# Delta projection of a state-space layer: scan work put between the sigmoids, one logarithm and one store in place of sixteen

## The chip, the cores and the metric

The program runs on all 8 cores of one Trainium2 chip. Each core takes one half of the sequence of one of the four batch rows, and runs the same instructions; nothing is exchanged between cores. The time is the device time of the slowest core, in microseconds (us). TensorE (PE) multiplies matrices, VectorE (DVE) does elementwise work and recurrences, ScalarE (ACT) does the activation functions, GpSimd (POOL) only issues stores here, and SyncE (SP) only issues loads. Each engine runs its own instructions in the order in which the program lists them.

## The reference, cut to what matters

```
x_and_res = x @ in_proj_w                       # 1024 -> 2 x 2048
h = silu(conv1d(xp) + conv_b)                   # depthwise, 4 taps
x_dbl = h @ x_proj_w                            # -> dlt (64), B (16), C (16)
delta = softplus(dlt @ dt_proj_w + dt_proj_b)   # 2048 channels
state_t = exp(delta_t * A) * state_{t-1} + delta_t * h_t * B_t
y = (state . C + h * D) * silu(res);   x1 = layernorm(x + y @ out_proj_w)
out = layernorm(x1 + shared_mlp(x1) + sum over the top 2 of 16 experts(x1))
```

The input is (4, 8192, 1024). The change touches only how `delta` is made and stored. The program keeps minus delta: ln(sigmoid(-v)) is -softplus(v).

## The kernel before, in words

A core owns 4096 tokens, but it also computes h, delta, B and C for the 4096 tokens ahead of them, since it needs the state with which its own half begins (a flag sets that state to zero on cores that hold the first half). The program has these stages, with a barrier of all engines between them: weights are cast to bf16; stage A makes h, delta, B, C and silu(res) for 32 slabs of 256 tokens (`SLAB`), the first 16 not owned, the last 16 owned; the scan stage runs the recurrence over the owned half; then output projection, norm, router, and the experts. Stage A runs from about 1014 us to the scan stage.

One slab of stage A goes as follows. SP loads x (L385 casts it on DVE). Then 16 column blocks, 32 where the slab is owned: PE multiplies (L403), DVE copies and does the four taps (L415 to L432), ACT applies Silu into `a_h` (L437); in an owned slab the second 16 blocks give silu(res), one activation (L445) and one store each. POOL stores h in one transfer of 2 MB. PE multiplies h by the 96 columns of `x_proj` (L455), ACT copies dlt, B and C out (L461, L464), POOL stores B and C. Then the part that is changed, which I call the delta part: a loop of 16 blocks with a matmul (L473) and a Sigmoid (L477) each, and a loop of 16 blocks with a Ln (L483) into one tile `a_dl` and a store to `d_delta` each. Ahead of each Ln, `QS.wait_all(sc)` makes ACT wait until all stores issued so far have landed, and so until `a_dl` may be written again.

Beside the slabs runs a generator, `gen_bp`, which works out what the half that is not owned leaves in the state. One instance covers 512 tokens, two slabs. Each call of `pump()` puts its next piece into the program at that point, on all engines. An instance has 16 pieces that spread B over the partitions (L311, L316), and then five for each of the 16 channel blocks (`dc`): the first loads delta and h, makes `b_u`, a running sum and `b_Dp` on DVE (L327, L329, L333), one small Exp (L337) and a group of four; the next three are a group of four each; the fifth adds to `sb_acc` (L362). A group of four is four Exp of 512 columns on ACT (L345), four products on DVE (L349) and four more with a sum (L355). The Exps of a group wait until the products L349 of the group before are done, by a wait of ACT on DVE. With the call that finds it finished, an instance takes 97 calls.

Before, `pump()` is called once ahead of each column block (16 or 32 calls a slab). An instance is made at the end of each odd slab among the first 16; what is left of it two slabs later is pumped out at once, which I call the drain (65 of 97 calls). The last instance, made after slab 15, has no drain and is worked off in the owned slabs 16 to 19. There are thus seven pairs of slabs with a drain (2 and 3 up to 14 and 15), and the first slab of a pair I call even, the second odd.

Of the kernel before, what the change touches and what calls it, by code (L numbers as in the profile page):

```python
# [11 lines left out]
AF = mybir.ActivationFunctionType  # L12
# [4 lines left out]
NDC = DIN // 128  # L17
NKC = DIM // 128
NF = 72
SLAB = 256  # L20
# [78 lines left out]
def build(T_OWN=4096, debug=False):  # L99
# [24 lines left out]
    out = nc.dram_tensor("out", [T_OWN, DIM], F32, kind="ExternalOutput").ap()  # L124
# [6 lines left out]
    def interior(name, shape, dt):  # L131
        return nc.dram_tensor(name, shape, dt, kind="Internal").ap()
# [6 lines left out]
    d_delta = interior("d_delta", [128, NDC, T2], F32)  # L139
# [39 lines left out]
    cx = Ctx(nc, es)  # L179
    te, sc, ve, sy, gp = nc.tensor, nc.scalar, nc.vector, nc.sync, nc.gpsimd  # L180
    QL = DmaQ(cx, sy, "qL", 8)
    QS = DmaQ(cx, gp, "qS", 8)

    with nc.Block() as blk:
        TE, SC, VE = "pTE", "pSC", "pVE"
# [79 lines left out]
        TE, SC, VE = "aTE", "aSC", "aVE"  # L265
# [8 lines left out]
        a_dl = A32.take(SLAB)  # L274
        a_sig = A32.take(NDC * SLAB)
# [94 lines left out]
        def pump():  # L370
            if pend[0] is not None:
                try:
                    next(pend[0])
                except StopIteration:
                    pend[0] = None
        for sl in range(2 * NS):
            t0 = sl * SLAB
# [4 lines left out]
                in_=x_fm_all[:, :, 8 + t0 - 3: 8 + t0 + SLAB].rearrange("k p c -> p k c"))  # L382
# [3 lines left out]
                                      in_=a_xfm.rearrange("p (k c) -> p k c", k=8)[:, :, 0:259]))  # L386
            x16_ready = cx.val(VE)
            m_list = list(range(16)) + (list(range(16, 32)) if owned else [])
            for mi, m in enumerate(m_list):
                pump()  # L390
                gi = (mi // 4) % 2
                if mi % 4 == 0:
                    cx.wait_val(sy, TE, wtb_free[gi])
                    QL.dma(out=wtb[gi].rearrange("p (k mc) -> p k mc", k=8),
                        in_=d_winb.rearrange("p (k mc) -> p k mc",
                                             k=8)[:, :, m * 128:(m + 4) * 128])
# [13 lines left out]
                if m < 16:  # L410
# [27 lines left out]
                                             in_=a_cv[1][:], func=AF.Silu,  # L438
                                             bias=sb_cb[:, dc:dc + 1]))
                    cv_rel[mi % 2] = cx.val(SC)  # L440
                else:
# [7 lines left out]
                                            in_=a_sil[:])  # L449
            cx.wait(gp, SC)  # L450
            QS.dma(out=d_h[:, :, t0:t0 + SLAB],
                                    in_=a_h.rearrange("p (d c) -> p d c", d=NDC))
# [14 lines left out]
            QS.dma(out=d_B[:, t0:t0 + SLAB], in_=a_bc[64:80, :])  # L467
            QS.dma(out=d_C[:, t0:t0 + SLAB], in_=a_bc[80:96, :])
            sig_rel = [0, 0]
            for m in range(NDC):  # L470
                pdt = pD if m % 2 == 0 else pC
                cx.wait_val(te, SC, max(sig_rel[m % 2], dlt_ready))
                cx.inc(TE, te.matmul(pdt[:, 0:SLAB], sb_wdt[:, m * 128:(m + 1) * 128],  # L473
                                     a_dlt[0:64, :], start=True, stop=True))
                cx.wait(sc, TE)
                cx.wait(sc, SC)
                cx.inc(SC, sc.activation(out=a_sig[:, m * SLAB:(m + 1) * SLAB], in_=pdt[:, 0:SLAB],  # L477
                                         func=AF.Sigmoid, scale=-1.0, bias=sb_ndtb[:, m:m + 1]))
                sig_rel[m % 2] = cx.val(SC)
            for m in range(NDC):  # L480
                QS.wait_all(sc)
                cx.wait(sc, SC)
                cx.inc(SC, sc.activation(out=a_dl[:], in_=a_sig[:, m * SLAB:(m + 1) * SLAB],  # L483
                                         func=AF.Ln))
                cx.wait(gp, SC)
                QS.dma(out=d_delta[:, m, t0:t0 + SLAB], in_=a_dl[:])

            if sl % 2 == 1 and sl < NS:
                while pend[0] is not None:
# [14 lines left out]
        TE, SC, VE = "oTE", "oSC", "oVE"  # L504
# [20 lines left out]
        for sl in range(NSB):  # L525
            t0 = T_OWN + sl * SLB
# [3 lines left out]
            for g in range(NST):  # L530
# [7 lines left out]
                                         in_=(pA if g % 2 == 0 else pB)[:, 0:SLB],  # L538
                                         func=AF.Copy))
            cx.wait(sy, TE)  # L540
            QL.dma(out=o_state[0:1, 0:NST * SLB], in_=d_C[:, t0:t0 + SLB])
            for g in range(NST):
# [7 lines left out]
                                         in_=(pA if g % 2 == 0 else pB)[:, 0:SLB],  # L550
                                         func=AF.Copy))
            for dc in range(NDC):
# [11 lines left out]
                for n0 in range(0, NST, 4):  # L564
                    cx.wait_val(sc, VE, dA_free[0])
                    for j in range(4):
                        cx.inc(SC, sc.activation(  # L567
                            out=o_dA[j][:], in_=o_dl[bb], func=AF.Exp,
                            scale=sb_negA[:, dc * NST + n0 + j:dc * NST + n0 + j + 1]))
                    cx.wait(ve, SC); cx.wait(ve, VE)  # L570
                    for j in range(4):
                        cx.inc(VE, ve.scalar_tensor_tensor(  # L572
                            out=o_dBu[j][:], in0=o_u[:], scalar=1.0,
# [3 lines left out]
                    for j in range(4):  # L577
                        n = n0 + j
                        cx.inc(VE, ve.tensor_tensor_scan(  # L579
                            out=o_state[:, n * SLB:(n + 1) * SLB], data0=o_dA[j][:],  # L580
# [5 lines left out]
                    for j in range(4):  # L586
                        n = n0 + j
                        cx.inc(VE, ve.scalar_tensor_tensor(  # L588
                            out=o_prod[j][:], in0=o_state[:, n * SLB:(n + 1) * SLB],
# [14 lines left out]
                    else:  # L604
# [8 lines left out]
                                          in_=o_state[:, SLB - 1::SLB]))  # L613
# [20 lines left out]
        TE, SC, VE = "cTE", "cSC", "cVE"  # L634
# [12 lines left out]
        for sl in range(NS):  # L647
            t0 = sl * SLAB
            cx.wait(sy, TE); cx.wait(sy, VE); cx.wait(sy, SC)
            QL.dma(out=c_y1.rearrange("p (d c) -> p d c", d=NDC),  # L650
                                    in_=d_y1[:, :, t0:t0 + SLAB])
            QL.dma(out=c_x.rearrange("p (a c) -> p a c", a=2),
                                    in_=x_own[t0:t0 + SLAB, :].rearrange("(a p) c -> p a c", p=128))
# [16 lines left out]
            for tc in range(2):  # L670
# [3 lines left out]
                for nh in range(2):  # L674
# [40 lines left out]
                                        in_=x1tc)  # L715
                for kc in range(NKC):
# [6 lines left out]
                        out=c_fm32[:, kc * SLAB + tc * 128:kc * SLAB + tc * 128 + 128],  # L723
                        in_=pC[:, 0:128], func=AF.Copy))
# [5 lines left out]
                                    in_=c_fm16.rearrange("p (k c) -> p k c", k=NKC))  # L730
            for tc in range(2):
                cx.wait(te, SC)
                for k in range(NKC):
# [52 lines left out]
                                         in_=pC[0:16, 0:128], func=AF.Copy))  # L786
# [4 lines left out]
        if debug:  # L791
            tmp = A32t[:, 0:DIM]
            for sl in range(NS):
                t0 = sl * SLAB
                for tc in range(2):
# [4 lines left out]
                                            in_=tmp)  # L800
# [4 lines left out]
                                        in_=tmp[0:16, 0:SLAB])  # L805
            stage_barrier([])

        TE, SC, VE = "dTE", "dSC", "dVE"
# [16 lines left out]
        for sl in range(NSD):  # L825
            t0 = sl * SLD
            cx.wait(sy, TE); cx.wait(sy, VE)
            QL.dma(out=g_x1.rearrange("p (k c) -> p k c", k=NKC),
                   in_=d_x1fm[:, :, t0:t0 + SLD])
            QL.dma(out=g_cwf[0:1, :], in_=d_cw[:, t0:t0 + SLD])  # L830
            for pe in range(18):
                pp = pe % 2
                f0 = pe * 4
                for g in range(2):
                    cx.wait_val(sy, TE, gwt_free[g][pp])
                    QL.dma(out=g_wt[g][pp].rearrange("p (k f c) -> p k f c", k=8, f=4),
                           in_=d_wgub.rearrange("g p (k ff c) -> g p k ff c",
                                                k=8, ff=NF)[g, :, :, f0:f0 + 4, :])
# [52 lines left out]
        TE, SC, VE = "eTE", "eSC", "eVE"  # L891
# [9 lines left out]
        for sl in range(NS):  # L901
            t0 = sl * SLAB
            cx.wait(sy, VE); cx.wait(sy, SC)
            QL.dma(out=e_x1.rearrange("p (a c) -> p a c", a=2),
                                    in_=d_x1[t0:t0 + SLAB, :].rearrange("(a p) c -> p a c", p=128))
            for half in range(2):
# [3 lines left out]
                                        in_=d_z[:, half * 36:(half + 1) * 36, t0:t0 + SLAB])  # L910
                for kk in range(36):
                    k = half * 36 + kk
                    gi2 = (kk // 2) % 2
                    if kk % 2 == 0:
                        cx.wait_val(sy, TE, ewd_free[gi2])
                        QL.dma(out=e_wd[gi2].rearrange("p (a c) -> p a c", a=2),
                               in_=d_wdownb[k:k + 2].rearrange("a p c -> p a c"))
# [17 lines left out]
            for tc in range(2):  # L935
# [3 lines left out]
                for nh in range(2):  # L939
# [24 lines left out]
                                         func=AF.Sqrt, scale=1.0 / DIM, bias=sb_tiny[:, 4:5]))  # L964
# [15 lines left out]
                                        in_=otc)  # L980
# [84 lines left out]
```

How the kernel before makes its waits and increments, by code:

```python
    def inc(self, name, instr, k=1):  # L39
        instr.then_inc(self.sem(name), k)
        self.ledger[name] += k
        return instr
# [4 lines left out]
    def wait_val(self, eng, name, v):  # L47
        if v <= 0:
            return
        key = (id(eng), name)
        if self.waited.get(key, -1) >= v:
            return
        eng.wait_ge(self.sem(name), v)
        self.waited[key] = v
```

## Time and profile before

| What | Value |
|---|---|
| Median of 3 runs | 26255.3 us (26250.2 to 26335.7) |
| The profiled execution's own time | 26236.4 us |
| Its span, first to last instruction, slowest core | 26234.9 us |
| Busy DVE / PE / ACT / POOL, share of the span | 45% / 28% / 19% / 4% |
| One pair of slabs with drain, 2058.3 to 2833.3 us | 775.0 us |
| One owned slab without a generator, from one store of h to the next | 188.3 us |

The span is that of the slowest of 8 cores (26186.8 to 26234.9 us). "Busy" counts an engine's own work, not its waits; in brackets behind a row of a timeline stands how long the engine stood idle ahead of it, and which engine or transfer ended that. No engine is busy half of the time, so the time lies in waits, and it has to be read stage by stage.

### The profile page before, as it was taken

The numbers are of one execution on the slowest core, as the hardware profiler recorded it, in microseconds if no ns is written. First come the engines' busy times: TensorE is split into PE (matmuls) and PEld (weight loads), VectorE is DVE, ScalarE is ACT, GpSimd is POOL, SyncE is SP. The second block draws the span as 40 slices with busy tenths as digits, with TensorE's granted clock in tenths as the row PEclk, the third lists the DMA queues.
The fourth block names the chain that finished last, engine by engine and source line by source line (L and its number), as shares of the span: only waits on it lengthen the run. The fifth ranks groups of instructions, "written<-read, shape, count | busy, mean of one in ns | idle before, by whom it ended". The sixth has DMA issues, their size and how long they took to land.

```text
span 26234.9 us, 118127 instructions; the slowest of 8 cores (26186.8 to 26234.9 us)
## 1 busy us (share of the span) xinstructions
PE 7269.4 (28%) x24864; PEld 3115.4 (12%) x24864; DVE 11884.3 (45%) x19992; ACT 5004.7 (19%) x8360; POOL 966.0 (4%) x1734
## 2 busy tenths in 40 slices
PE   0112211102234442000000000000233577775444
PEld 0101100001112221000000000000111233332111
DVE  1255565655532124877877878778200122220000
ACT  0033333333431111111111111111111111110000
POOL 0000000000001110000000000000000011100000
PEclk9855555555555555555555555555555688988888
DMA  5411111011122221000000000000111233334555
GB/s 207 146 35 39 38 35 40 30 32 37 52 65 82 87 82 42 15 14 14 16 13 14 16 13 15 15 13 16 50 59 59 92 127 126 124 127 153 165 169 163
DMA packets 1154022, 1729.76 MB, mean 66 GB/s; under 512 B 66272, under 2 KB 780512, under 8 KB 1141984
## 3 DMA queue, kind: packets, MB, share of 16 engines
q1 hardware_dynamic: 1039360, 1349.58, 16.3%
q0 software_dynamic: 113952, 372.62, 3.9%
q8 instruction: 213, 3.49, 0.1%
q14 instruction: 497, 4.07, 0.1%
HBM read 1349.44 MB, written 372.51 MB: 66 GB/s over the span
## 4 chain that ended last, share of the span: by engine, by line
DVE 40%; DMA 27%; PE 11%; ACT 11%; issue 9%; DVEq 1%; SPq 0%; ACTq 0%; POOLq 0%; POOL 0%
DVE A L579 9%; DMA d_z<-A 6%; DMA A<-d_wdownb 5%; DVE A L588 5%; DVE A L572 5%; ACT A L345 5%; DVE A L349 5%; DMA d_delta<-A 4%; DMA A<-d_woutb 3%; PE pO L924 3%; DMA d_silu<-A 2%; DVE A L355 2%; PE pO L663 2%; DVE A L593 1%; DVE A L874 1%
## 5 line engine op out<-in xcount | busy, mean ns | idle before, releaser
L579 DVE TENSOR_TENSOR_SCAN A<-A,sb_carry 128x512 f32<-128x512 f32 x2048 | 2463.0, 1264 | 55.0 <-DVE A L572 1.8
L567 ACT ACTIVATE A<-A,sb_negA 128x512 f32<-128x512 f32 x2048 | 1310.2, 710 | 6097.5 <-DVE A L579 3485.4
L532 PE MATMUL pA<-A,sb_ones 1*128 1x512 f32 x128 | 130.7, 1122 | 6746.3 <-DMA A<-d_B 6699.4
L349 DVE SCALAR_TENSOR_TENSOR A<-A 128x512 f32<-128x512 f32 x2048 | 1278.9, 687 | 1561.4 <-ACT A L345 1561.4
L572 DVE SCALAR_TENSOR_TENSOR A<-A 128x512 f32<-128x512 f32 x2048 | 1279.1, 686 | 642.6 <-ACT A L567 601.7
L924 PE MATMUL pO<-A 128*128 128x512 bf16 x4608 | 1173.7, 403 | 1282.9 <-DMA A<-d_wdownb 1282.8
L403 PE MATMUL pA<-A 128*128 128x259 bf16 x3072 | 713.9, 412 | 2665.0 <-DMA A<-d_winb 1288.6
L345 ACT ACTIVATE A<-A,sb_A 128x512 f32<-128x512 f32 x2048 | 1307.7, 709 | 738.1 <-DVE A L349 736.8
L854 PE MATMUL pO<-A 128*128 128x512 bf16 x4608 | 1238.0, 417 | 546.5 <-DVE A L874 545.2
L355 DVE SCALAR_TENSOR_TENSOR A<-A 128x512 f32<-128x512 f32 x2048 | 1295.2, 689 | 54.3 <-DVE A L349 0.9
L870 DVE SCALAR_TENSOR_TENSOR A<-pO,A 128x512 f32<-128x512 f32 x512 | 354.2, 692 | 2100.2 <-DMA d_z<-A 1772.6
L588 DVE SCALAR_TENSOR_TENSOR A<-A 128x512 f32<-128x512 f32 x2048 | 1279.1, 687 | 54.9 <-DVE A L579 1.8
L403 PE MATMUL pB<-A 128*128 128x259 bf16 x3072 | 715.5, 412 | 1698.5 <-DVE A L415 1405.3
L863 PE MATMUL pO<-A 128*128 128x512 bf16 x4608 | 1164.0, 398 | 0.0
L311 PE MATMUL pO<-A,sb_ones 1*128 1x512 f32 x256 | 262.0, 1125 | 2873.7 <-DMA A<-d_B 2441.7
L941 DVE TENSOR_TENSOR A<-pO,A 128x512 f32<-128x512 f32 x64 | 44.3, 692 | 2238.4 <-PE pO L924 1933.9
L663 PE MATMUL pO<-A 128*128 128x512 bf16 x1024 | 477.4, 620 | 1803.0 <-DMA A<-d_woutb 1803.0
L532 PEld LDWEIGHTS pA<-A,sb_ones 1*128 1x128 f32 x128 | 31.8, 307 | 6844.3 <-issue 6844.3
L860 ACT ACTIVATE A<-pO 128x512 f32<-128x512 f32 x576 | 344.0, 597 | 2234.6 <-PE pO L854 2234.6
L403 PEld LDWEIGHTS pA<-A 128*128 128x128 bf16 x3072 | 395.7, 138 | 3050.9 <-issue 2902.2
L676 DVE TENSOR_TENSOR A<-pO,A 128x512 f32<-128x512 f32 x64 | 44.3, 692 | 1515.9 <-PE pO L663 1185.8
L385 DVE CAST A<-A 128x2072 bf16<-128x2072 f32 x32 | 39.8, 1242 | 1522.5 <-DMA A<-x_fm_all 1522.5
(146 smaller groups left out, 11420.2 us busy)
## 6 DMA issues: line engine op xcount, KB each, us to landing
A<-d_wgub SPq DMA_DIRECT2D x288, 1024.0 KB, 8.0
A<-d_wdownb SPq DMA_DIRECT2D x576, 512.0 KB, 3.7
A<-d_winb SPq DMA_DIRECT2D x192, 1024.0 KB, 6.4
A<-wgu_f SPq DMA_DIRECT2D x36, 2048.0 KB, 7.2
d_z<-A POOLq DMA_DIRECT2D x576, 128.0 KB, 2.0
A<-d_z SPq DMA_DIRECT2D x32, 2304.0 KB, 14.6
d_h<-A POOLq DMA_DIRECT2D x32, 2048.0 KB, 9.0
d_delta<-A POOLq DMA_DIRECT2D x512, 128.0 KB, 2.0
```

Of the source, the lines that this page charges most:

```text
L345: cx.inc(BSC, sc.activation(out=b_E[j][:], in_=b_Dp[:], func=AF.Exp, scale=sb_A[:, dc * NST + n0 + j:dc * NST + n0 + j + 1]))
L349: cx.inc(BVE, ve.scalar_tensor_tensor(out=b_w[j][:], in0=b_E[j][:], scalar=1.0, in1=b_u[:], op0=OP.mult, op1=OP.mult))
L355: cx.inc(BVE, ve.scalar_tensor_tensor(out=b_wb[j][:], in0=b_w[j][:], scalar=1.0, in1=b_brep[:, (n0 + j) * SLB:(n0 + j + 1) * SLB], op0=OP. ...
L403: ins = te.matmul(ps[:, 0:259], wtb[gi][:, (k * 4 + mi % 4) * 128:(k * 4 + mi % 4 + 1) * 128], x16[:, k * 264:k * 264 + 259], start=(k == ...
L567: cx.inc(SC, sc.activation(out=o_dA[j][:], in_=o_dl[bb], func=AF.Exp, scale=sb_negA[:, dc * NST + n0 + j:dc * NST + n0 + j + 1]))
L572: cx.inc(VE, ve.scalar_tensor_tensor(out=o_dBu[j][:], in0=o_u[:], scalar=1.0, in1=o_brep[:, (n0 + j) * SLB:(n0 + j + 1) * SLB], op0=OP.mul ...
L579: cx.inc(VE, ve.tensor_tensor_scan(out=o_state[:, n * SLB:(n + 1) * SLB], data0=o_dA[j][:], data1=o_dBu[j][:], initial=sb_carry[:, dc * NS ...
L588: cx.inc(VE, ve.scalar_tensor_tensor(out=o_prod[j][:], in0=o_state[:, n * SLB:(n + 1) * SLB], scalar=1.0, in1=o_crep[:, n * SLB:(n + 1) * ...
L663: ins = te.matmul(pO[tc * 2 + nh][:, 0:512], c_y1[:, k * SLAB + tc * 128:k * SLAB + tc * 128 + 128], wb[:, nh * 512:(nh + 1) * 512], start ...
L854: ins = te.matmul(pg[:, 0:SLD], g_wt[0][pp][:, (k * 4 + f) * 128:(k * 4 + f + 1) * 128], g_x1[:, k * SLD:(k + 1) * SLD], start=(k == 0), s ...
L863: ins = te.matmul(pu[:, 0:SLD], g_wt[1][pp][:, (k * 4 + f) * 128:(k * 4 + f + 1) * 128], g_x1[:, k * SLD:(k + 1) * SLD], start=(k == 0), s ...
L924: ins = te.matmul(pO[tc * 2 + nh][:, 0:512], e_z[hb][:, kk * SLAB + tc * 128:kk * SLAB + tc * 128 + 128], wb[:, nh * 512:(nh + 1) * 512], ...
```

## The change: one wait moved, 20 more pieces a slab, one logarithm and one store

Ahead of the Sigmoid loop ACT now waits for all stores. In the loop each block begins with a `pump()`; one more follows the loop, then a single Ln over all 16 blocks (4096 columns, in place in `a_sig`), a single store of 2 MB, and three more calls of `pump()`. A slab thus makes 20 more calls while a generator is alive.

```
             QS.dma(out=d_C[:, t0:t0 + SLAB], in_=a_bc[80:96, :])
             sig_rel = [0, 0]
+            QS.wait_all(sc)
             for m in range(NDC):
+                pump()
                 pdt = pD if m % 2 == 0 else pC
...
                 sig_rel[m % 2] = cx.val(SC)
-            for m in range(NDC):
-                QS.wait_all(sc)
-                cx.wait(sc, SC)
-                cx.inc(SC, sc.activation(out=a_dl[:], in_=a_sig[:, m * SLAB:(m + 1) * SLAB],
-                                         func=AF.Ln))
-                cx.wait(gp, SC)
-                QS.dma(out=d_delta[:, m, t0:t0 + SLAB], in_=a_dl[:])
+            pump()
+            cx.wait(sc, SC)
+            cx.inc(SC, sc.activation(out=a_sig[:, :], in_=a_sig[:, :], func=AF.Ln))
+            cx.wait(gp, SC)
+            QS.dma(out=d_delta[:, :, t0:t0 + SLAB],
+                   in_=a_sig.rearrange("p (d c) -> p d c", d=NDC))
+            pump(); pump(); pump()
```

On ACT, in the delta part of slab 2 (the first even slab), the two copies of dlt, B and C (L461, L464), then the Sigmoids stood in a row before:

```order
L461 ACTIVATE A<-pC 64x256 [waits aTE,qS0,aSC]
L464 ACTIVATE A<-pC 32x256 [waits aSC]
L477 ACTIVATE A<-pD,sb_ndtb 128x256 [waits aTE,aSC]
L477 ACTIVATE A<-pC,sb_ndtb 128x256 [waits aTE,aSC]
L477 ACTIVATE A<-pD,sb_ndtb 128x256 [waits aTE,aSC]
```

The Sigmoids waited for TensorE alone (aTE) and for ACT's own last write. Now, in the same kind of place in the odd slab 3 (the Sigmoid is L479 now, bVE is the generator's DVE):

```order
L461 ACTIVATE A<-pC 64x256 [waits aTE,qS6,aSC]
L464 ACTIVATE A<-pC 32x256 [waits aSC]
L345 ACTIVATE A<-A,sb_A 128x512 [waits qS0,qS7,bVE]
L345 ACTIVATE A<-A,sb_A 128x512 x3
L479 ACTIVATE A<-pD,sb_ndtb 128x256 [waits aTE,aSC]
L345 ACTIVATE A<-A,sb_A 128x512 [waits bVE]
L345 ACTIVATE A<-A,sb_A 128x512 x3
L479 ACTIVATE A<-pC,sb_ndtb 128x256 [waits aTE,aSC]
```

Groups of four Exps stand between the Sigmoids; the wait for the two stores (qS0, qS7) is ahead of the first group, and the Sigmoids' own waits are the same as before. At the end of the same delta part ACT now has this row of work, the last Sigmoid, a group, the one Ln (L484), and groups again:

```order
L479 ACTIVATE A<-pC,sb_ndtb 128x256 [waits aTE,aSC]
L345 ACTIVATE A<-A,sb_A 128x512 [waits bVE]
L345 ACTIVATE A<-A,sb_A 128x512 x3
L484 ACTIVATE A<-A 128x4096 [waits aSC]
L345 ACTIVATE A<-A,sb_A 128x512 [waits bVE]
L345 ACTIVATE A<-A,sb_A 128x512 x3
L337 ACTIVATE A<-sb_negA,A 128x16 [waits bVE,bSC]
L345 ACTIVATE A<-A,sb_A 128x512 x4
```

The Ln waits for nothing but ACT itself, and the group behind it waits for the generator's DVE and for no store. On DVE, at the end of slab 2's taps (L432), stood the cast of the next slab's x (L385), and only then the first piece of a channel block (L327 to L333):

```order
L432 SCALAR_TENSOR_TENSOR A<-A,sb_cw 128x256 [waits aVE]
L385 CAST A<-A 128x8x259 [waits qL0,qL1,qL2,qL3,qL4,qL7,aVE]
L327 SCALAR_TENSOR_TENSOR A<-A 128x512 [waits qL5,qL6]
L329 SCALAR_TENSOR_TENSOR A<-sb_ones,A 128x512
L333 TENSOR_SCALAR A<-A 128x512 [waits bVE]
```

Now the piece stands right behind the taps, with four channel blocks ahead of the cast:

```order
L432 SCALAR_TENSOR_TENSOR A<-A,sb_cw 128x256 [waits aVE]
L327 SCALAR_TENSOR_TENSOR A<-A 128x512 [waits qL0,qL1,qL2,qL3,qL4,qL5,qL7]
L329 SCALAR_TENSOR_TENSOR A<-sb_ones,A 128x512
L333 TENSOR_SCALAR A<-A 128x512 [waits bVE]
L340 TENSOR_TENSOR A<-sb_acc,A 128x16 [waits bSC]
L349 SCALAR_TENSOR_TENSOR A<-A 128x512 [waits bSC,bVE]
```

DVE has the same instructions in all; they only stand elsewhere. (The order's name for L329 is that of the profile's TENSOR_TENSOR_SCAN.)

## Rows read from the trace of the kernel before

**Rows 1.** Windows: us, busy (xinstructions) of PE, PEld, DVE, ACT, POOL; PEclk; DMA; GB/s

```profile
2058.28:2833.25 774.97, 142.06 (x416) 70.67 (x416) 441.38 (x1011) 259.39 (x418) 21.74 (x38) 0.51 0.11 36
6874.60:7253.60 379.00, 85.82 (x326) 48.49 (x325) 186.04 (x428) 164.83 (x229) 19.59 (x36) 0.51 0.17 51
7253.60:7624.30 370.70, 84.14 (x318) 47.14 (x317) 180.17 (x416) 159.71 (x223) 19.56 (x36) 0.51 0.17 51
7813.60:8001.90 188.30, 81.30 (x318) 46.24 (x317) 39.11 (x81) 33.11 (x69) 19.47 (x35) 0.54 0.27 83
```

**Rows 2.** Waits of ACT, 1010 to 9480 us: us in total, times, longest

```profile
ACT A L483 <- DMA d_delta<-A: 1322.2, 420, 9.6
```

**Rows 3.** Timeline of ACT, slab 21: start, us, what, [idle before <-releaser]

```profile
8201.27 0.38 ACT L461 ACTIVATE A<-pC 64x256 f32<-64x256 f32 x1 [12.20 <-DMA d_h<-A]
8201.74 0.38 ACT L464 ACTIVATE A<-pC 32x256 f32<-32x256 f32 x1
8203.58 1.28 ACT L477 ACT_TABLE_LOAD   x1 [1.47 <-PE pD L473]
...
8220.00 1.28 ACT L483 ACT_TABLE_LOAD   x1
8221.29 0.42 ACT L483 ACTIVATE A<-A 128x256 f32<-128x256 f32 x1
8228.22 0.42 ACT L483 ACTIVATE A<-A 128x256 f32<-128x256 f32 x1 [6.51 <-DMA d_delta<-A]
...
8278.87 1.28 ACT L437 ACT_TABLE_LOAD   x1 [2.70 <-DMA d_delta<-A]
```

**Rows 4.** Timeline of POOL, the same slab: stores as they are issued

```profile
8191.90 1.14 POOL L75 DMA_DIRECT2D d_h<-A  x1 [1.70 <-issue]
...
8203.23 0.50 POOL L75 DMA_DIRECT2D d_C<-A  x1
```

**Rows 5.** Timeline of DVE, the slab after it: end of its second block's taps

```profile
8235.98 0.48 DVE L432 SCALAR_TENSOR_TENSOR A<-A,sb_cw 128x256 f32<-128x256 f32 x1
```

**Rows 6.** The page's DMA issues: KB each, us from issue to landing

```profile
d_C<-A POOLq DMA_DIRECT2D x32, 16.0 KB, 1.7
```

**Rows 7.** Groups of ACT by line, whole span: busy, mean ns of one, idle before

```profile
L681 ACT ACTIVATE A<-A 128x1024 f32<-128x1024 f32 x32 | 33.8, 1056 | 1420.0 <-DVE A L676 1420.0
```

**Rows 8.** Timeline of DVE and ACT in the drain of slab 7

```profile
3323.11 2.50 DVE L349 SCALAR_TENSOR_TENSOR A<-A 128x512 f32<-128x512 f32 x4 [0.18 <-ACT A L345]
...
3328.44 2.50 DVE L349 SCALAR_TENSOR_TENSOR A<-A 128x512 f32<-128x512 f32 x4 [0.19 <-ACT A L345]
...
3336.53 0.31 ACT L337 ACTIVATE A<-sb_negA,A 128x16 f32<-128x16 f32 x1 [8.26 <-DVE A L333]
...
3339.46 2.50 DVE L349 SCALAR_TENSOR_TENSOR A<-A 128x512 f32<-128x512 f32 x4 [2.34 <-ACT A L345]
...
3363.52 0.31 ACT L337 ACTIVATE A<-sb_negA,A 128x16 f32<-128x16 f32 x1 [8.27 <-DVE A L333]
```

**Rows 9.** Timeline of ACT, slabs 4 and 5: delta parts and taps

```profile
2144.13 0.38 ACT L464 ACTIVATE A<-pC 32x256 f32<-32x256 f32 x1
...
2219.04 0.42 ACT L483 ACTIVATE A<-A 128x256 f32<-128x256 f32 x1 [2.72 <-DMA d_delta<-A]
2219.36 0.29 ACT L337 ACTIVATE A<-sb_negA,A 128x16 f32<-128x16 f32 x1
...
2233.44 2.56 ACT L345 ACTIVATE A<-A,sb_A 128x512 f32<-128x512 f32 x4
2244.16 1.28 ACT L437 ACT_TABLE_LOAD   x1 [8.16 <-DVE A L432]
...
2245.98 1.28 ACT L345 ACT_TABLE_LOAD   x1
2247.28 2.56 ACT L345 ACTIVATE A<-A,sb_A 128x512 f32<-128x512 f32 x4
...
2420.61 0.38 ACT L464 ACTIVATE A<-pC 32x256 f32<-32x256 f32 x1
```

## The prediction

> **What bounds the kernel now.** I read the slices of the page first: DVE is the busiest engine at 45%, so the span is made of waits. Then I cut stage A into windows. A pair of slabs with a drain takes 775.0 us, of which DVE works 441 and ACT 259; an owned slab without a generator takes 188.3 us, with DVE at 39 and ACT at 33 [rows 1]. In both most of the time belongs to no engine. The list of ACT's waits names the owner of much of it: ACT waited 1322 us, 420 times, for a `d_delta` store to land before it could write the next Ln into the one tile [rows 2]. The timeline of one delta part shows the pattern: a Ln of 0.42 us, then a wait of 2.7 to 6.5, sixteen times; from the table load of the Ln to that of the next slab's Silu 58.9 us go by [rows 3]. The last view is the drain, where DVE is full: groups follow each other every 5.33 us (3323.11 to 3328.44), of which 0.19 are idle, and a channel block takes 26.99 us (3336.53 to 3363.52) [rows 8]. So there are three kinds of place: delta parts with no generator, where only latency is lost; delta parts with one alive, during which DVE's generator work could run; and drains, which DVE bounds and which get shorter by what is done earlier.
>
> The sum is made against the profiled execution, 26236.4 us (span 26234.9). That is 19 us under the median of the runs, which I add at the end.
>
> **Term 1: 16 delta parts with no generator work beside them** (slabs 0, 1 and 18 to 31; slab 18 still had pieces before, and they come under term 3).
> Before: from the end of L464 (8202.12) to the Silu's table load (8278.87), 76.75 us [rows 3].
> After, step by step:
> - The wait for the B and C stores now stands ahead of the Sigmoids. The second is issued at 8203.23, 1.1 us after L464 ends, and such a store lands in 1.7 [rows 4, 6], so the first table load comes after 2.8; I take 3.0 where it was 1.47. Cost 1.5.
> - The Sigmoid loop is the same, 8203.58 to 8220.00: 16.4.
> - Ln: load 1.28, then 4096 columns. 256 columns take 0.42 [rows 3] and 1024 take 1.06 [rows 7], so 0.83 us for 1000 columns, and 3.6 for all. Together 4.9, of which sixteen small ones would have used 6.7 for the same columns; the gain is in the waits.
> - The store: 0.6 to its issue (the first half of the 1.1 above, which holds two issues), then as the store of h, which has the same shape and size: issued at 8191.90, ACT released at 8201.27, 9.4 us [rows 3, 4]. That one ran nearly alone. This one meets the loads of the next slab's x and weights. Their price can be bounded by the first Ln wait after them, 6.51 where the last is 2.70 [rows 3]: 3.8, and I allow nearly twice that, 7, since this store has sixteen times the bytes. So 9.4 to 16.4; I take 14, near the upper end, since all of it falls among these loads.
> Sum 3.0 + 16.4 + 4.9 + 0.6 + 14 = 38.9, and 76.75 − 38.9 = 37.8; I use 37.5, with 35 to 42.5 as ends. Next in line are the taps of the slab that follows: two blocks of them were ready at 8236.46, 16.5 us after the Sigmoids ended (8220.00) [rows 3, 5], and the Silu now comes 19.5 after them. So the taps are just not late; if the store were quicker than 11 us, they would be what ends the wait. For slab 1 (whose end is followed by a wait of SP) and slab 31 (followed by the barrier), the loads matter less: 42 each. Term 1: 14 × 37.5 + 2 × 42 = 609 us.
>
> By the Trainium skill (DMA: Bandwidth & Descriptors, section Anatomy of one DMA — SWDGE (gpsimd) path) such a store takes 2.0 us plus its bytes over 436 KB per us, 6.8 us for 2 MB. The row above has 9.4, so it does not agree; by the rule term 1 would be about 42 us larger.
>
> **Term 2: seven pairs with a drain.** The generator's pieces are only moved: 20 into the even slab, 20 into the odd, 40 fewer in the drain. In the delta part a group now stands between two Sigmoids. The Sigmoid waits for TensorE and not for DVE, so ACT does its table load and the Sigmoid (1.28 + 0.47) while DVE does its four products L349 (2.50); that is hidden. Not hidden is the load ahead of the next Exps, since it comes behind the wait for these products: 1.28, with the gap 1.30 (2245.98 to 2247.28) [rows 9]. A group costs 5.33 + 1.30 = 6.63, and a channel block with four such loads 27.0 + 5.2 = 32.2. No load stands between a Ln and an Exp (2219.04, 2219.36) [rows 9]. The single Ln, 4.9 us, stands where ACT else waits 2.8 for DVE, so it costs 2.1. Whether Exp next to Sigmoid needs a load is not in the trace; each costs 0 or 1.3 by the rows, and I take 1.3 as between Silu and Exp.
> Even slab, from the end of L464 to the first Exp of the fifth block (L337): before 2144.51 to 2219.36, 74.9. After: store wait 3.0; three blocks 96.6; the fourth with two loads and the Ln 27.0 + 2.6 + 2.1 = 31.7; the cast of x, which is now in DVE's row of work, 1.3. Sum 132.6. Cost 57.7. The odd slab's taps begin at the same piece as before, so they take the same time.
> Odd slab, from the end of L464 (2420.99) to the end of the pair (2833.25): before 412.3 [rows 1, 9]. After: wait 3.0; first group to its products 1.3 + 2.6 + 0.2 = 4.1; from there to the next L337, two groups (2 × 5.33) and 8.1 (3328.44 to 3336.53), plus 2.6 of loads, 21.4; two blocks 64.4; one with three loads and the Ln 33.0; five in the drain 135.0; less 2.1, because the drain ends ahead of the next block's first steps. Sum 258.8. Gain 153.5.
> A pair gains 95.8; I use 95: term 2 is 665 us.
>
> **Term 3: slabs 16 to 18.** Slab 16's delta part now takes 20 pieces. From L464 to the first group of slab 17 it is 3.0 + 4.1 + 21.4 + 64.4 + 33.0 + 5.5 (from L337 over its own group to the next, 2.9 + 2.6) = 131.4, against 74.9 in the like part before: cost 56.5. Slab 17 takes 32 pieces in its blocks as before (379.0 and 370.7 us for such slabs [rows 1]), and the last 12 in its delta part: wait 3.0, group 4.1, to L337 8.1, a block 32.2, the last block to its fourth products 2.9 + 1.3 + 3 × 6.63 = 24.1, the last Sigmoids 6, Ln 4.9, issue and store 14, so 96.4, 20 more than 76.75. Slab 18 is then free of pieces: 188.3 + 20 in place of 370.7, gain 162. Term 3: 162 − 56.5 = 106; I use 105.
>
> Sum: 609 + 665 + 105 = 1379. 26236.4 − 1379 = 24857, plus 19: 24876, and I say 24880 us, 5.2% faster. The later stages have the same instructions, and the scan stage is bound by DVE; I give them nothing. The change leaves ACT with 480 fewer Ln and POOL with 480 fewer stores; beyond the waits counted above I give that nothing.
>
> **A rule that speaks against this.** In the row, a load of 1.28 at 2244.16, a Silu and a load of 1.28 at 2245.98 are all done by 2247.28: 3.12 us, which leaves 0.56 for the Silu and every gap [rows 9]. So a switch costs 1.3 here. The Trainium skill (ScalarE: Activation LUTs, section What ACT_TABLE_LOAD costs) puts a switch at 2.66 us, 1.38 of it a drain beside the load. By the rule each load on the path would cost twice as much; the time is that of the third rival.
>
> **The rivals.**
> - *The moved pieces gain nothing* (terms 2 and 3 are zero, term 1 stands): stalls that I don't see, of loads for the generator behind the next x in SP's queue or of stores, eat 95 us a pair. For it: ACT is ordered, and the generator was slow in the taps. Against it: the delta part has no DVE work of its own. Time 26255 − 609 = 25646.
> - *The delta part runs at the pace of the taps, and the kernel is slower.* In the taps a group takes 13.84 us (2233.44 to 2247.28), because ACT's Silu waits for DVE (8.16 idle at 2244.16) and the next Exps stand behind it [rows 9]. If the Sigmoid were held as long, a group would cost 7.2 more. 26 groups a pair and 22 in term 3 are 204 groups: 1469 us, more than 1379. Time 26255 + 90 = 26345. It decides from 6.63 + 1379/204 = 13.4 us a group. Against it: the Sigmoid's wait is on TensorE, whose matmul is ready two blocks ahead.
> - *A switch costs 1.38 us more in the delta part*, by a drain of ACT that the Silu rows don't show. On the path are 28 loads a pair (14 in each slab) and 23 in term 3: 219 × 1.38 = 302. Time 25180.
> - *Exp and Sigmoid need no load between them*: 219 × 1.3 = 285 us more gain. Time 24595.
>
> **How the numbers follow.** My forecast 0.83, nothing from the moved pieces 0.05, slower 0.03, dearer switches 0.05, no loads 0.04. My own terms have these ends: term 1 from 560 to 680, term 2 from 75 to 105 us a pair, so 525 to 735, and with term 3 as it is they leave 24735 to 25065. The range 24730 to 25100 holds these and leaves the rivals out. A measurement of this kernel tells about 0.3% (79 us) from no change. Faster by more than that: all but the slower rival and a small rest, 0.95; within 0.3%: 0.02; slower 0.03.
>
> **What would show it.** One Ln of 3.6 us a slab, and ACT's wait for `d_delta` gone from 1322 us to some 10 us in 14 to 16 places, now ahead of a Silu. In the delta parts of slabs 2 to 17, DVE's products L349 every 6.6 us with a table load of L345 ahead; a spacing of 5.3 would speak for the last rival, 8 for the third, 13 for the second. A pair of 680 us, with a drain of 25 pieces. An owned slab without generator of 151 us. If slabs without generator don't get shorter by 35 or more, the wait on the store was not what held them, and the forecast fails at its first term.

## The result: 5.6% faster, and the profile after

| | before | after |
|---|---|---|
| Median of 8 runs each | 26266.2 us | 24803.7 us |
| Ratio, 95% interval | | 0.9441 [0.9431, 0.9451] |
| Profiled execution, its span | 26236.4, 26234.9 us | 24812.4, 24810.6 us |
| ACT's wait for `d_delta` stores inside the delta part, core 4, all of stage A | 1502 us, 476 times | none |

The forecast was 24880 us; the measured time is 76 us lower and inside the range. The slowest core was core 2 before and is core 4 after; so that two dies are not mixed up, I compare core 4 of both. [rows 2] are of core 2 and end at 9480 us, before the stage does, hence the 1322 us there. On core 4 the waits of ACT before, and what is left after, now ahead of the next slab's Silu:

```profile
ACT A L483 <- DMA d_delta<-A: 1502.2, 476, 8.7
...
ACT L437 <- DMA d_delta<-A: 133.2, 10, 16.6
```

The prediction had 14 to 16 such places of some 10 us. There are 10, of 13.3 us on average; in most of the other delta parts without a generator DVE's taps end the wait, which the prediction called just not late.

The stage can be cut at the stores of h. The timeline of POOL on core 4 before, at slabs 2, 16, 18 and 31:

```profile
1364.24 1.14 POOL L75 DMA_DIRECT2D d_h<-A  x1 [77.50 <-ACT A L437]
...
6863.07 1.18 POOL L75 DMA_DIRECT2D d_h<-A  x1
...
7608.71 1.18 POOL L75 DMA_DIRECT2D d_h<-A  x1
...
10032.68 1.14 POOL L75 DMA_DIRECT2D d_h<-A  x1 [1.70 <-issue]
```

and after, at the same four slabs:

```profile
1282.58 1.13 POOL L75 DMA_DIRECT2D d_h<-A  x1 [85.92 <-ACT A L437]
...
6105.30 1.13 POOL L75 DMA_DIRECT2D d_h<-A  x1 [0.56 <-issue]
...
6742.37 1.17 POOL L75 DMA_DIRECT2D d_h<-A  x1
...
8640.36 1.17 POOL L75 DMA_DIRECT2D d_h<-A  x1
```

The differences give the account, beside what the prediction had for each piece (slab 0's own store of h stands at 1075.9 before and 1070.2 after; the first matmul of the scan stage at 10117.2 and 8688.7):

| Stretch, core 4 | before | after | gain | predicted |
|---|---|---|---|---|
| h of slab 0 to h of slab 2 | 288.4 | 212.4 | 76.0 | 79.5 (term 1) |
| slab 2 to slab 16 (the seven pairs) | 5498.8 | 4822.7 | 676.1 | 665 (term 2) |
| slab 16 to slab 18 | 745.6 | 637.1 | 108.5 | 105 (term 3) |
| slab 18 to slab 31 | 2424.0 | 1898.0 | 526.0 | 487.5 (term 1) |
| slab 31 to the scan stage | 84.5 | 48.3 | 36.2 | 42 (term 1) |

With the 5.7 us ahead of slab 0, which the change does not touch (that store stands anywhere from 1060 to 1076 in the ten profiles), stage A got 1428.5 us shorter, where 1379 was forecast. The stages behind it took 9 us longer in this execution, with the same instructions. The windows of the kernel after (core 4; columns as in [rows 1]) for a pair, the slabs from 16 and from 17, and an owned slab without generator:

```profile
1614.03:2289.16 675.13, 144.80 (x417) 70.52 (x416) 441.47 (x1010) 317.19 (x438) 6.61 (x8) 0.51 0.13 41
...
6105.30:6538.18 432.88, 85.61 (x321) 47.51 (x320) 274.81 (x636) 235.46 (x307) 11.94 (x20) 0.51 0.16 49
6538.18:6742.37 204.19, 85.21 (x322) 47.89 (x321) 92.42 (x208) 75.30 (x109) 12.70 (x21) 0.53 0.25 80
6888.77:7033.72 144.95, 81.10 (x322) 46.28 (x321) 39.40 (x81) 30.08 (x54) 11.98 (x22) 0.56 0.34 109
```

DVE's work in a pair is what it was in [rows 1] (441 us), so the 100 us by which this pair is shorter were idle time of DVE. ACT has 20 more instructions, with 30 fewer Ln, so 50 more table loads: 64 us, less 6 for the Lns, and its work grew from 259 to 317. The delta part of a slab without generator, on ACT (answers to [rows 3]):

```profile
6898.09 0.38 ACT L464 ACTIVATE A<-pC 32x256 f32<-32x256 f32 x1
6901.46 1.28 ACT L479 ACT_TABLE_LOAD   x1 [3.00 <-DMA d_C<-A]
...
6917.89 1.28 ACT L484 ACT_TABLE_LOAD   x1
6919.18 3.62 ACT L484 ACTIVATE A<-A 128x4096 f32<-128x4096 f32 x1
6936.29 1.28 ACT L437 ACT_TABLE_LOAD   x1 [13.49 <-DMA d_delta<-A]
```

From the end of L464 (6898.47) to the Silu's load are 37.8 us; 38.9 was forecast and 76.75 stood there before. Over the 13 slabs from 18 to 30 the mean is 37.8, where it was 77.5 before; a store ends the wait in nine of them and the taps in four. The Ln takes 3.62 where 3.6 was worked out, the wait for the small stores 3.00 where I took 3.0. And with a generator alive, on ACT at the end of slab 4's delta part (answers to [rows 8, 9]):

```profile
2072.63 0.47 ACT L479 ACTIVATE A<-pC,sb_ndtb 128x256 f32<-128x256 f32 x1
2074.07 1.28 ACT L345 ACT_TABLE_LOAD   x1 [0.96 <-DVE A L349]
2075.36 2.56 ACT L345 ACTIVATE A<-A,sb_A 128x512 f32<-128x512 f32 x4
2077.82 3.60 ACT L484 ACTIVATE A<-A 128x4096 f32<-128x4096 f32 x1
2081.33 2.54 ACT L345 ACTIVATE A<-A,sb_A 128x512 f32<-128x512 f32 x4
```

and DVE a little ahead of it:

```profile
2052.59 2.50 DVE L349 SCALAR_TENSOR_TENSOR A<-A 128x512 f32<-128x512 f32 x4 [1.46 <-ACT A L345]
...
2059.19 2.50 DVE L349 SCALAR_TENSOR_TENSOR A<-A 128x512 f32<-128x512 f32 x4 [1.46 <-ACT A L345]
```

The products follow each other every 6.60 us (6.63 was forecast), idle 1.46 in place of 0.19: a table load stands ahead of each group of Exps. The Ln has none ahead of it when it follows an Exp, which I had not seen coming (the load before the Exps already brings the logarithm); it saves 1.3 us in each such delta part.

### The profile page after: what moved, and what is told of

Same layout as the page of the kernel before. It is cut to its first block, busy times and chain, and to the rows that moved or that the text cites. A ratio compares the mean times of both kernels' runs of the same rounds, so it can differ in the third digit from the quotient of the medians.

```text
span 24810.6 us, 115616 instructions; the slowest of 8 cores (24748.5 to 24810.6 us)
## 1 busy us (share of the span) xinstructions
PE 7561.1 (30%) x24864; PEld 3166.4 (13%) x24864; DVE 11887.1 (48%) x19992; ACT 5347.4 (22%) x8224; POOL 725.2 (3%) x1254
## 4 chain that ended last, share of the span: by engine, by line
DVE 43%; DMA 24%; PE 12%; ACT 12%; issue 8%; DVEq 1%; SPq 0%; ACTq 0%; POOLq 0%; POOL 0%
DVE A L581 10%; DMA d_z<-A 6%; DMA A<-d_wdownb 6%; DVE A L590 5%; DVE A L574 5%; DVE A L349 5%; ACT A L345 5%; DMA A<-d_woutb 3%; PE pO L926 3%; DMA d_silu<-A 2%; DVE A L355 2%; PE pO L665 2%; DVE A L595 1%; DVE A L876 1%; DVE A L872 1%
## 5 line engine op out<-in xcount | busy, mean ns | idle before, releaser
L926 PE MATMUL pO<-A 128*128 128x512 bf16 x4608 | 1184.0, 405 | 1299.7 <-DMA A<-d_wdownb 1299.4
L856 PE MATMUL pO<-A 128*128 128x512 bf16 x4608 | 1344.1, 445 | 276.8 <-DVE A L876 272.4
L355 DVE SCALAR_TENSOR_TENSOR A<-A 128x512 f32<-128x512 f32 x2048 | 1295.5, 689 | 55.3 <-DVE A L349 2.3
L865 PE MATMUL pO<-A 128*128 128x512 bf16 x4608 | 1307.7, 436 | 0.0
L665 PE MATMUL pO<-A 128*128 128x512 bf16 x1024 | 477.6, 621 | 1800.1 <-DMA A<-d_woutb 1800.1
L926 PEld LDWEIGHTS pO<-A 128*128 128x128 bf16 x4608 | 437.1, 102 | 2046.7 <-issue 1684.3
L385 DVE CAST A<-A 128x2072 bf16<-128x2072 f32 x32 | 41.3, 1290 | 1294.4 <-DMA A<-x_fm_all 1013.2
```

Source lines behind the costliest of these rows:

```text
L355: cx.inc(BVE, ve.scalar_tensor_tensor(out=b_wb[j][:], in0=b_w[j][:], scalar=1.0, in1=b_brep[:, (n0 + j) * SLB:(n0 + j + 1) * SLB], op0=OP. ...
L665: ins = te.matmul(pO[tc * 2 + nh][:, 0:512], c_y1[:, k * SLAB + tc * 128:k * SLAB + tc * 128 + 128], wb[:, nh * 512:(nh + 1) * 512], start ...
L856: ins = te.matmul(pg[:, 0:SLD], g_wt[0][pp][:, (k * 4 + f) * 128:(k * 4 + f + 1) * 128], g_x1[:, k * SLD:(k + 1) * SLD], start=(k == 0), s ...
L865: ins = te.matmul(pu[:, 0:SLD], g_wt[1][pp][:, (k * 4 + f) * 128:(k * 4 + f + 1) * 128], g_x1[:, k * SLD:(k + 1) * SLD], start=(k == 0), s ...
L926: ins = te.matmul(pO[tc * 2 + nh][:, 0:512], e_z[hb][:, kk * SLAB + tc * 128:kk * SLAB + tc * 128 + 128], wb[:, nh * 512:(nh + 1) * 512], ...
```

## The experiments

My sum was right in its total, but it did not say which edit earned it: the pairs' 665 us stood in a term that speaks of moved pieces. Theory A: the gain is the sixteen waits on a store, also where a generator is alive, and the moved pieces little more than pay for their table loads. Theory B: in pairs and slabs 16 to 18 the moved pieces earn it. All medians below are of 4 runs and stand against the kernel before, timed on the same chip. Its median was 26271.8 us beside experiments 1 to 4, 26238.3 beside 5 to 7 and 26256.2 beside 8, so a difference of medians across these groups carries some 30 us that are not the kernel's. A pair is the mean of six, from the h store of slab 3 to that of slab 15, on core 4: 770.4 us before, 673.6 in the changed kernel.

**1. The single Ln and the single store, without the extra pieces.**

```
             for m in range(NDC):
-                pump()
                 pdt = pD if m % 2 == 0 else pC
...
-            pump()
             cx.wait(sc, SC)
...
-            pump(); pump(); pump()
```

> The changed kernel without the 20 extra pieces: one wait ahead of the Sigmoids, one Ln of 4096 columns and one store stay, the generator is pumped only in the taps as before the change. Theory A (nearly all of the gain is the sixteen waits on a store, with or without a generator beside them; the moved pieces about pay for their own table loads): from the end of L464 to the next L337 about 30 us in an even slab (75 before), 25 to the next group in an odd one (69 before), so a pair with drain takes 686 us (775 before, 675 in the changed kernel), and the time is about 24900 us, 0.4% above the changed kernel. Theory B (as my sum could be read: what pairs and slabs 16 to 18 gained comes from the moved pieces): a pair stays near 775 us, time about 25590 us.

Measured: 24910.6 us, ratio 0.9484 [0.9470, 0.9498]. A pair takes 686.2 us. The delta part of slab 4 on ACT:

```profile
1984.87 0.37 ACT L464 ACTIVATE A<-pC 32x256 f32<-32x256 f32 x1
...
2005.92 3.62 ACT L482 ACTIVATE A<-A 128x4096 f32<-128x4096 f32 x1
2018.01 0.31 ACT L337 ACTIVATE A<-sb_negA,A 128x16 f32<-128x16 f32 x1 [8.48 <-DVE A L333]
```

L464 to L337 is 32.8 us where 74.9 stood [rows 9], and the generator does not wait for the store at all: only the next Silu does, and it comes later. DVE, in the same slab, shows what the old waits did to the generator: its small product L340 waits for an Exp of ACT (L337) that stood behind the sixteen Lns, so DVE was idle for 46.92 us in the kernel before, and for 0.56 here.

```profile
2218.73 0.17 DVE L340 TENSOR_TENSOR A<-sb_acc,A 128x16 f32<-128x16 f32 x1 [46.92 <-ACT A L337]
...
2018.42 0.18 DVE L340 TENSOR_TENSOR A<-sb_acc,A 128x16 f32<-128x16 f32 x1 [0.56 <-ACT A L337]
```

Theory B is out. Of the 96.8 us that a pair gained, 84.2 come without any moved piece; the pieces add 12.6, and over the whole program 107 us (0.9484 against 0.9441).

**2. The pieces alone.** The kernel before, with `pump()` at the head of each Sigmoid block, one behind the loop and three behind the sixteen stores; Ln, stores and waits as before.

```
             for m in range(NDC):
+                pump()
                 pdt = pD if m % 2 == 0 else pC
...
+            pump()
             for m in range(NDC):
                 QS.wait_all(sc)
...
                 QS.dma(out=d_delta[:, m, t0:t0 + SLAB], in_=a_dl[:])
+            pump(); pump(); pump()
```

> The kernel before with the 20 extra pieces alone: 16 in the Sigmoid loop, one behind it, three at the end; the sixteen Ln with a store and a wait each stay. Theory A: the delta part of an even slab gets 108 us longer and that of an odd one with its drain 105 us shorter, a pair stays within 10 us of 775, slabs 16 to 18 gain some 25 us; time 26230 to 26280 us, no change. Theory B: DVE's idle time in the Sigmoid loops is filled and the drain shrinks by 216 us a pair; time about 25500 us.

Measured: 26130.1 us, ratio 0.9950 [0.9935, 0.9965], 0.5% faster where I had no change. A pair takes 756.8 us, 13.6 less, not within 10; slabs 16 to 18 gained 24.7, as expected. What I missed stands in the Ln loop of slab 4:

```profile
2226.91 0.40 ACT L485 ACTIVATE A<-A 128x256 f32<-128x256 f32 x1
2230.09 0.42 ACT L485 ACTIVATE A<-A 128x256 f32<-128x256 f32 x1 [2.77 <-DMA d_delta<-A]
...
2274.23 0.42 ACT L485 ACTIVATE A<-A 128x256 f32<-128x256 f32 x1 [2.71 <-DMA d_delta<-A]
2274.55 2.54 ACT L345 ACTIVATE A<-A,sb_A 128x512 f32<-128x512 f32 x4
```

The loop takes 47.6 us where I had put 55: the first wait is 2.77, and there is no table load ahead of it. In the kernel before the same loop of slab 4 took 55.9 us from its first Ln to L337 (2218.34), because two waits were long:

```profile
2162.47 0.42 ACT L483 ACTIVATE A<-A 128x256 f32<-128x256 f32 x1
2170.80 0.42 ACT L483 ACTIVATE A<-A 128x256 f32<-128x256 f32 x1 [7.91 <-DMA d_delta<-A]
2177.03 0.42 ACT L483 ACTIVATE A<-A 128x256 f32<-128x256 f32 x1 [5.82 <-DMA d_delta<-A]
```

So an even slab grew by 98 us and not by 108, and an odd one shrank by 111 and not by 105. Theory B (25500 us) is far off; theory A's small worth of the pieces (12.6 in the first experiment, 13.6 here) holds; I had expected less still.

**3. Exp and Ln(1 + x) in place of Sigmoid and Ln.** What limits the pieces should be the table load between Sigmoid and Exp. This kernel has the same pieces and almost the same instructions, without the switch:

```
-  func=AF.Sigmoid, scale=-1.0, bias=sb_ndtb[:, m:m + 1]
+  func=AF.Exp, scale=1.0, bias=sb_dtb[:, m:m + 1]
...
-  sc.activation(out=a_sig[:, :], in_=a_sig[:, :], func=AF.Ln)
+  sc.activation(out=a_sig[:, :], in_=a_sig[:, :], func=AF.Ln, bias=1.0)
...
   # delta is now positive: b_u and o_u with scalar=-1.0, the running sum with
   # op1=OP.subtract, the scan stage's Exp with scale=sb_A
```

> The changed kernel with the Sigmoid replaced by an Exp of dt plus its bias and the Ln by Ln(1 + x), so that delta is stored with a plus sign; the signs of the two products u, of the running sum and of the scan stage's scale are turned to match. Same number of instructions, but Exp, Ln and the generator's Exp should need no table load between them. My term for a load on the path (1.3 us, 28 a pair, 23 in slabs 16 to 17, and one ahead of each Ln in the 16 delta parts without pieces) gives 253 + 30 + 21 = 304 us less: 24500 us, a group every 5.33 us in the delta part, a pair of 638 us. If a load's cost is hidden by DVE: 24780 us. If a switch costs 2.66 us: 24190 us.

Measured: 24551.6 us, ratio 0.9347 [0.9331, 0.9363]; 1.0% under the changed kernel. A pair takes 640.7 us, 32.9 less. DVE in the delta part of slab 4:

```profile
2003.11 2.50 DVE L349 SCALAR_TENSOR_TENSOR A<-A 128x512 f32<-128x512 f32 x4 [0.18 <-ACT A L345]
2008.43 2.50 DVE L349 SCALAR_TENSOR_TENSOR A<-A 128x512 f32<-128x512 f32 x4 [0.18 <-ACT A L345]
```

5.32 us from one to the next: the delta part runs at the pace of the drain, and the 1.3 us was the table load. I had counted 28 loads a pair; the first of each delta part stays, since a Silu is ahead of it, so 26 go: 32.9 / 26 = 1.27 us each. Slabs 16 to 18 gained 28.9 (30 expected). The 21 us of the parts without generator did not come: a slab takes 146.9 us against 146.0, and the delta part (L464 to the Silu's load, mean of 13 slabs) 38.0 against 37.8, though its Ln has no load. The taps end the wait in six of the 13 here and in four there; why they come later is not shown. Both rivals are out. The pairs (230 us in place of 253) and these 21 make up 44 of the 52 us between my 304 and the measured 252.

**4. The same without the extra pieces** (the first experiment with the third's activations; no other edit).

> The Exp and Ln(1 + x) form without the 20 extra pieces (the first experiment with the third's activations). Only one table load a delta part falls away, 32 x 1.3 = 42 us: about 24860 us. With the third experiment it gives the worth of the moved pieces when they pay for no table load: 24860 - 24500 = 360 us, where it is some 95 us with Sigmoid. Theory B would have it near 25550 us.

Measured: 24893.5 us, ratio 0.9478 [0.9464, 0.9492]; a pair 682.7 us. That is 17 us under the first experiment, where I had expected 42: a pair gained 3.5 us (2.6 expected), and the slabs without generator again nothing (145.6 us against 145.7), as in the third. So the pieces are worth 342 us (24893.5 − 24551.6) and 42.0 us a pair when no switch stands between them, against 107 and 12.6 with Sigmoid. Interleaving earned a third of what it could, because it put two functions of different tables side by side: in a pair 32.9 us for the 26 loads and 12.6 make 45.5, against 42.0 and the 3.5 that the form brings by itself.

**5. The taps' Silu one block later**, on top of the third. It is written behind the next piece's Exps; `silu_held()` holds the Silu as it was, with its waits:

```
             for mi, m in enumerate(m_list):
                 pump()
+                if held:
+                    silu_held()      # Silu of the block before
...
-                    cx.wait(sc, VE); QS.wait_all(sc)
-                    ... Silu into a_h ...
+                    held.append((mi, dc, a_cv, cx.val(VE)))
```

> The third experiment (Exp and Ln(1 + x), all pieces) with the taps' Silu of each block written one block later, behind the generator's next Exps instead of ahead of them. In the taps a group now takes 13.84 us because ACT's Silu waits for DVE's taps with the Exps behind it. With the Silu late, DVE should go from the taps straight to the next products: about 8.3 us a group with its block's taps. 13 groups a pair and 13 in slab 17, with some 4 us kept at each first piece: 53 us a pair, 425 us in all, 24130 us. If what holds the groups there is not this order, the time stays near 24550 us.

Measured: 24044.7 us, ratio 0.9163 [0.9149, 0.9177]. A pair takes 580.5 us, 60 less (53 expected), and slabs 16 to 18 gained 59. That makes 483 us, as the ratios do (0.9347 less 0.9163), where 425 were expected; the medians alone give 507. ACT in the taps of an odd slab (L395 is the Silu):

```profile
2073.72 2.56 ACT L345 ACTIVATE A<-A,sb_A 128x512 f32<-128x512 f32 x4
2077.84 1.28 ACT L395 ACT_TABLE_LOAD   x1 [1.56 <-DVE A L445]
...
2080.20 1.28 ACT L345 ACT_TABLE_LOAD   x1 [0.55 <-DVE A L349]
2081.49 2.56 ACT L345 ACTIVATE A<-A,sb_A 128x512 f32<-128x512 f32 x4
```

A group with its taps takes 7.77 us in place of 13.84 [rows 9]. Both switches are still there, but now they lie beside DVE's work and cost nothing: DVE's products follow each other every 7.76 us and no idle time stands ahead of them.

```profile
2077.63 2.49 DVE L349 SCALAR_TENSOR_TENSOR A<-A 128x512 f32<-128x512 f32 x4
...
2085.39 2.49 DVE L349 SCALAR_TENSOR_TENSOR A<-A 128x512 f32<-128x512 f32 x4
```

In the kernel before, DVE stood idle 6.04 us ahead of the same products (core 4, 2235.15). This is also the check on my second rival: the pace of the taps really came from the Silu that waits for DVE ahead of the Exps.

**6. The same kernel once more.** The label speaks of a ring of tiles; the kernel has none, it is the fifth again.

> One look at the kernel of the run ahead once more, for the spread from run to run of its windows: within 0.3% of it.

Measured: 24042.8 us in its one run, a pair 580.3 us. So a pair's mean repeats within 0.2 us.

**7. The Silu waits for the store of h alone.** The changed kernel with one wait narrowed:

```
-                    cx.wait(sc, VE); QS.wait_all(sc)
+                    cx.wait(sc, VE)
+                    if h_dma[0] is not None:
+                        cx.wait_val(sc, *h_dma[0])
...
+            nm = QS.names[(QS.i - 1) % QS.n]     # behind the store of h
+            h_dma[0] = (nm, cx.val(nm))
```

> The changed kernel where the taps' Silu waits only for the store of h that reads its tile, and no longer for the delta store. My reading of slabs without generator: the delta store holds the Silu until 36 us after L464, and the taps of two blocks are ready at 33 and 36, so only 2 to 3 us are to be had: 13 slabs, some 30 us, 24775 us. If the store were what still bounds the delta part, the 13.5 us of the wait would come off: 24630 us.

Measured: 24744.6 us, ratio 0.9431 [0.9415, 0.9447]. The interval overlaps that of the changed kernel, so the times alone don't tell; the windows do: 143.5 us a slab without generator against 146.0, 32 us in 13 slabs, where 30 were expected. (The medians differ by 59 us and the ratios by 26.) The Silu's releaser has changed:

```profile
6919.15 3.62 ACT L488 ACTIVATE A<-A 128x4096 f32<-128x4096 f32 x1
6931.60 1.28 ACT L439 ACT_TABLE_LOAD   x1 [8.83 <-DVE A L432]
```

The first Silu of this slab starts 4.7 us earlier (4.3 in the mean of 13), held by the taps in all of them and no longer by the store, and the slab keeps 2.5 of it. So the store of 2 MB was the last to end, but the taps stood close behind it, as the prediction had it.

**8. The best version: the fifth, with that narrowed wait and four tiles for silu(res).**

```
-        a_sil = A32.take(SLAB)
+        a_silr = [A32.take(SLAB) for _ in range(4)]
...
-                    cx.wait(sc, TE); QS.wait_all(sc)
+                    a_sil = a_silr[dc % 4]
+                    cx.wait(sc, TE)
+                    if sil_dma[dc % 4] is not None:
+                        cx.wait_val(sc, *sil_dma[dc % 4])
```

> The fifth kernel with two waits narrowed: the taps' Silu waits only for the store of h, and silu(res) is written to four tiles in turn, each waiting only for its own last store (before: one tile, and a wait for all stores, 3.1 us a block where the matmuls need about 2). An owned slab without generator takes 146 us; its second sixteen blocks should fall from 53 to about 31 us, and 2 to 3 come at its start: 24 us a slab, 14 slabs, some 340 us: 23700 us. If those blocks are bound by TensorE or by the weights' loads already, the gain is under 100 us: 23950 us.

Measured: 23586.7 us, ratio 0.8982 [0.8967, 0.8997]. A slab without generator takes 111.7 us (146.0 before this edit, 122 expected), and silu(res) now waits mostly for its matmul (19 waits for a store in 13 slabs, 194 in the fifth kernel):

```profile
6036.29 0.38 ACT L459 ACTIVATE A<-pA 128x256 f32<-128x256 f32 x1 [1.71 <-PE pA L419]
6038.02 0.38 ACT L459 ACTIVATE A<-pB 128x256 f32<-128x256 f32 x1 [1.35 <-PE pB L419]
```

It is 4.9% under the changed kernel by the two medians. It gained more than I had expected (458 us against the fifth, 340 expected). The second sixteen blocks of a slab fell from 55.3 to 22.8 us (mean of slabs 19 to 30), 1.4 us a block where I had put 2; that is the 10 us a slab that I had not counted. The two edits were not run apart on this kernel; the start of the slab, which the narrowed wait concerns, came forward by 2.6 us.

## Why the prediction was right

- *Slabs without generator (term 1, 609 us forecast, 638 measured).* Right step by step; the size that was most off is the store. I took 0.6 to its issue and 14 more, from bounds of 9.4 and 16.4; the wait was 13.5 in all, 3.5 over the lower bound and its issue, half of what I allowed. Loads of x and weights were issued from 6917.36 to 6935.88 beside it, but no run takes them away, so that they cost the 3.5 us is not shown. Over the 13 slabs the delta part fell by 39.7 us, where I had 37.5, and a slab by 40.5. Slab 1 and the end of stage A, which I put at 42 us each as free of contention, gave 35.4 and 36.2; what else stands there I have not shown.
- *Pairs (term 2, 665 forecast, 676 measured).* A group at 6.60 us, a channel block at 32.1 (2035.17 to 2067.27 on ACT), the Ln beside DVE's products: all as worked out. Both halves fit too: from one store of h to the next the even slab's delta part cost 56.3 us (57.7 forecast) and the odd one's with its drain gained 153.1 (153.5). The 14 loads ahead of an Exp in each delta part are there. The Ln's own load is absent: with the Ln the Exps follow after 5.97 us in place of 5.33 (2075.36 to 2081.33), so it costs 0.6 and not 2.1. Of the 11 us, 6 are my rounding of 95.8 to 95. In the prices of the last two rivals the 28 loads a pair were two too many, since the first in each delta part is needed after a Silu in any case.
- *Slabs 16 to 18 (term 3, 105 forecast, 108.5 measured).* Right in both parts: 55.3 us more behind slab 16 (56.5) and 163.9 less behind slab 17 (162).
- *What the prediction left open.* Term 2 begins with the words that the pieces are only moved, and its account is of them; but of the 96.8 us a pair, 84.2 come without moving any. Its sum was right all the same, since it set whole stretches before against whole stretches after. The rival "the moved pieces gain nothing" was priced at 25646 us, as if terms 2 and 3 would then be zero. The first experiment is that case, and it runs at 24911. The waits on the stores lay on the path in the pairs as well, and only an experiment with one edit at a time split the two. That is a fault of that rival's price, which left term 1's mechanism out of the pairs, not of the sum.
- *The slower rival* failed by its condition: the Sigmoid does wait for TensorE alone. *The dearer switch* is out: 1.27 us by the third experiment, where the Trainium skill (ScalarE: Activation LUTs, section What ACT_TABLE_LOAD costs) would have 2.66. *No load between Exp and Sigmoid* is out: the rows show one each way.
- *The 76 us.* Against the profiled executions the forecast gain was 1379 and the measured one 1424. The other 31 us lie in how a profiled execution stands to its median: I had added 19 us for that (and 4 by rounding), while the profiled execution of the changed kernel ran 9 us above its own median.

## What to carry to other kernels

When an activation writes one tile that a store must empty, the price is the store's latency times the number of blocks; one large store costs far less than the sum of the small ones, here 13.5 us in place of sixteen waits of 2.7 to 7.9. When independent work is put between the instructions of an engine that runs in order, look at two things: what the neighbour's function needs (a switch of tables on the path cost 1.3 us each time, and in all two thirds of what the moved pieces could have earned), and whether an instruction that waits stands ahead of one that others wait for. Both are cured by writing order and algebra, not by more overlap: they brought some 750 us here (759 by the medians, 730 by the ratios), and narrowed waits with four tiles another 460.

## What the runs showed of the hardware

- A Ln that follows an Exp had no table load ahead of it, and an Exp that follows a Ln neither (2075.36 to 2081.33 above). The Trainium skill (ScalarE: Activation LUTs, section Table sets: the hidden batching unit) says that one set holds both; the trace agrees. With softplus as Ln(1 + Exp) the whole delta part needs one load, and the third experiment's 252 us come from that.
- A store of 2 MB in rows of 1 KB took 13.5 us from the end of the Ln to ACT's release beside other loads, 12.9 of them from its issue on POOL (6923.42). By the rule that the prediction cites (6.8 us) it would have been half; the measurement decides.
- The same loop of sixteen small stores took 55.9 us in the kernel before and 47.6 in the second experiment, with nothing in the stores changed. The longer waits were the first ones. The loads of x and weights were issued as the loop began in the one, and 15 us ahead of it in the other (core 4; the first Ln stands at 2162.47 and 2226.91). That they are the cause was not tested:

```profile
2160.66 0.38 SPq L75 DMA_DIRECT2D A<-x_fm_all  x1
...
2211.41 0.38 SPq L75 DMA_DIRECT2D A<-x_fm_all  x1
```
